# Two instead of three products of the cleared tile at the head of TensorE's program

## What is computed

```python
x = x + _L0_xattn_ref(_layernorm(x), ctx_768, Wq, Wk, Wv, Wo, bo)        # 8 heads of 64
x = x + _L0_ffn_ref(_layernorm(x), ...)                                  # 16 experts, 4 of them chosen in groups, one shared
x = x + _L1_xattn_ref(_layernorm(x), ctx_768, Wq, Wk, Wv, Wo)            # 16 heads of 8
x = x + _L1_ffn_ref(_layernorm(x), ...)                                  # 8 experts, 2 chosen, one shared
```

## Time and profile before

| | |
|---|---|
| median of three runs | 231.79 us |
| the three runs | 231.2, 231.79, 233.03 us |
| the profiled execution, first to last instruction | 230.0 us |
| PE busy | 223.5 us, 97% |
| DVE, ACT, POOL busy | 163.7, 155.3, 126.4 us |

### The profile page before, as it was taken

The page is one execution under the profiler, slowest core; times in us unless marked ns, Lnnn a source line. Parts: engine busy times, 40 slices in busy tenths (PEclk is TensorE's granted clock), DMA queues, the critical chain, the costliest instruction groups (busy, mean ns, idle before and its releaser), DMA issues.

```text
span 230.0 us, 4315 instructions
## 1 busy us (share of the span) xinstructions
PE 223.5 (97%) x1389; PEld 166.7 (72%) x1389; DVE 163.7 (71%) x480; ACT 155.3 (68%) x378; POOL 126.4 (55%) x127
## 2 busy tenths in 40 slices
PE   7999999999999999999999999999999999999994
PEld 3676765965889898889535563588878887888883
DVE  3589984788667863699948983564857775776874
ACT  2579999986679445672689778876365586745561
POOL 2765743899046937767492107209499400996540
PEclk9999999999999999999999999999999999999999
DMA  6890000000029925900600000028000003700002
GB/s 204 211 296 4 1 3 0 0 3 1 3 74 242 362 114 144 221 3 4 217 3 3 3 1 6 0 79 293 0 0 0 3 0 87 284 0 4 0 0 91
DMA packets 10172, 17.04 MB, mean 74 GB/s; under 512 B 3715, under 2 KB 5540, under 8 KB 9766
## 3 DMA queue, kind: packets, MB, share of 16 engines
q1 hardware_dynamic: 9926, 16.45, 23.5%
q10 hardware_dynamic: 224, 0.32, 0.4%
HBM read 16.08 MB, written 0.62 MB: 73 GB/s over the span
## 4 chain that ended last, share of the span: by engine, by line
PE 86%; ACT 6%; DVE 4%; POOL 2%; issue 1%; DVEq 0%; POOLq 0%
PE psum L1175 12%; PE psum L1179 11%; PE psum L1176 11%; PE psum L1348 7%; ACT prob L749 5%; PE psum L1410 5%; PE psum L1356 4%; PE psum L1358 3%; PE psum L1357 3%; PE psum L1466 3%; PE psum L1294 3%; PE psum L1306 3%; PE psum L1431 2%; PE psum L1270 2%; PE psum L1183 2%; PE psum L1454 2%
## 5 line engine op out<-in xcount | busy, mean ns | idle before, releaser
L703 POOL TENSOR_TENSOR act_s<-act_s,spread 128x512 f32<-128x512 f32 x35 | 44.3, 1293 | 20.2 <-DMA spread<-cw 14.5
L1175 PE MATMUL psum<-xT_hi,w_hi 128*128 128x512 f32 x108 | 43.9, 406 | 0.0
L1179 PE MATMUL psum<-xT_lo,w_hi 128*128 128x512 f32 x108 | 42.3, 392 | 0.0
L1176 PE MATMUL psum<-xT_hi,w_lo 128*128 128x512 f32 x108 | 42.2, 391 | 0.0
L798 ACT CAST q<-psum 128x512 fp32r<-128x512 f32 x35 | 20.4, 587 | 20.4 <-PE psum L1358 14.1
L1009 DVE TENSOR_TENSOR q<-psum,q 128x512 fp32r<-128x512 f32 x35 | 23.8, 687 | 13.5 <-ACT q L798 13.2
L788 ACT ACTIVATE act_s<-psum 128x512 f32<-128x512 f32 x39 | 23.0, 597 | 12.3 <-PE psum L1179 7.7
L1146 DVE TENSOR_REDUCE neg_max<-psum 128x2 f32<-128x308 f32 x64 | 26.2, 472 | 4.3 <-PE psum L1410 4.0
L703 POOL TENSOR_TENSOR hid<-hid,spread 128x512 f32<-128x512 f32 x13 | 16.6, 1296 | 18.9 <-DMA spread<-cw 14.6
L652 POOL TENSOR_TENSOR rstd<-vareps,minus_half 128x4 f32<-128x4 f32 x8 | 8.1, 1017 | 34.0 <-DVE vareps L910 34.0
L646 POOL TENSOR_TENSOR w_lo<-w_src,w_hi 128x768 fp32r<-128x768 f32 x12 | 21.7, 1830 | 8.3 <-ACT w_hi L718 8.3
(11 more groups left out here) (171 smaller groups left out, 469.6 us busy)
## 6 DMA issues: line engine op xcount, KB each, us to landing
spread<-cw SPq DMA_DIRECT2D x16, 256.0 KB, 4.9
spread<-cw SPq DMA_DIRECT2D x6, 512.0 KB, 5.7
w_src<-in_w SPq DMA_DIRECT2D x2, 1152.0 KB, 5.1
w_src<-in_w SPq DMA_DIRECT2D x1, 2304.0 KB, 11.6
spread<-cw SPq DMA_DIRECT2D x8, 128.0 KB, 3.0
w<-in_w SPq DMA_DIRECT2D x1, 576.0 KB, 6.6
out<-X SPq DMA_DIRECT2D x4, 128.0 KB, 1.8
wv<-in_wv SPq DMA_DIRECT2D x2, 192.0 KB, 4.7
```

Of the source, the lines that this page charges most:

```text
L703: pool.tensor_tensor(g, g, spread[:, slot, :], ALU.mult).then_inc(weighed, 1)
L1175: pe.matmul(dst, w_hi, xT_hi[:, b, :], start=True, stop=False)
L1176: pe.matmul(dst, w_lo, xT_hi[:, b, :], start=False, stop=False)
L1179: return pe.matmul(dst, w_hi, xT_lo[:, b, :], start=False, stop=True)
```

## The change

The third product of the cleared tile, the one of 256 columns, is left out. The wait for `idle_ready`, the bank and everything behind it stay as they are.

```diff
             pe.wait_ge(idle_ready, 1)
-            for n in (TOK, TOK, TOK // 2):
+            for n in (TOK, TOK):
                 pe.matmul(psum[:, 7, 0:n], act_s[:, 0, 0:P], act_s[:, 0, 0:n], start=True, stop=True)
```

## The result

The changed kernel takes 232.43 us (median of 20 runs), the kernel before 231.56 in as many: ratio 1.004, 95% interval 1.0026 to 1.0054. The forecast was 231.4. The time is inside the stated range (230.7 to 233.3), but the sign is wrong: the change costs 0.9 us where 0.4 was to be won.

The account below looks back on a forecast made before the run. PE, busy 97% of the span, was taken to bound the kernel, its first third at half rate. The lead of 0.41 us less 0.02 at batch 1's transposes gave 0.4: 231.79 to 231.4 us, range 230.7 to 233.3.

Parts of the forecast that it names:

- PE's head is on the path, and the load of wk is late next.: Kernel start: cleared products lie on the chain; without the third, kT waits for wk's load and starts at 5.10 us.
- Nobody reads bank 7 and no semaphore hangs on it, so nothing else goes with it.: Removed product: only 0.85 us of slow PE time goes, with no other effect.
- a lead was there at 15 us and gone at the end: Sign of a wrong prediction: PE's gain, expected to last to the end, seen at 15 us and then lost.
- The rise of the clock at 7.5 us.: During kT: PE goes from 1.2 to 2.4 GHz at a fixed 7.5 us, leaving 0.41 us of the 0.76 us lead.
- The forecast's gain: Whole kernel: 0.4 us faster, 231.4 us; chance 0.5.
- the whole lead remains: Rival at kT: clock rises with the work, PE keeps 0.76 us, gain hardly over 0.5, 231.2 us; chance 0.1.
- the clock rises later: Rival ahead of kT: PE's idle gap delays the clock's rise, 1.1 to 2.1 us slower, 232.9 to 233.9; chance 0.2.
- the lead is eaten: Rival: late wk or vf1 load, or batch 1's tile, leaves 0 to 0.2 us of gain, 231.7 us; chance 0.2.

Follow-up runs that it names:

- e4: Third product left out and the first kT made to wait for the identity's load too, against the kernel before: ratio 1.0077.
- e1: The same change run once more (products of 512, 512 columns), against the kernel before: ratio 1.004.
- f2: Third product left out, four PE instructions given back behind the store by two extra transposes at cwT of batch 1, against the kernel before: ratio 1.0053.
- g1: All three products kept, four PE instructions removed at about 52.5 us (low part of x skipped for two first-gate tiles), against the kernel before: ratio 1.0047.
- g3: Third product left out, two PE instructions given back by doing one transpose of the first xT twice, against the kernel before: ratio 1.0027.
- f1: Third product left out, four PE instructions given back ahead of the store by doubling a small vs product (about 21 us), against the kernel before: ratio 0.9997.
- e2: Third product cut from 256 to 8 columns, as many instructions as before, against the kernel before: ratio 1.0007.
- f4: One product of 512 columns and two of 8, as many instructions as before, against the kernel before: ratio 1.006.

## Why the prediction was wrong, point by point

- *PE's head is on the path, and the load of wk is late next.* Right. The first pass of kT started at 4.81 to 5.07 in the traces with two products that had no added wait, where 5.0 to 5.2 was expected.
- *"Nobody reads bank 7 and no semaphore hangs on it, so nothing else goes with it."* This step failed. Four instructions went with it, and everything behind them moved up in PE's program. The refill that used to run at 60.9 us, ahead of the store of the routing weights, ran at 64.0 to 64.8 (66.1 in e4, whose head is 1.4 us later), on top of it, in every run with two to four instructions less at that point (the change, e1, e4, f2, g1, g3), and the store took 3.16 to 3.59 us there against 1.83 to 1.85 in the six others. f1 and f2 differ in where the four instructions come back (and in what small product brings them), and g1 has the loss without the head. This is shown. Two rows more leave little room for another cause: in all six the first of the five late packets starts within 0.02 us of the refill's end, and the next store of the same size, at 84 to 87 us, takes 1.81 to 1.84 in all twelve traces. In the recorded pair the store lands 1.3 us later, and PE goes from 0.15 us ahead to 0.6 behind: a lead was there at 15 us and gone at the end, one of the signs that the prediction gave for being wrong. That the five packets queued behind the refill on one engine is read from their number, a sixteenth of 80, and from their start at its end; the engine's name isn't in the trace.
- *Why two instructions move the refill by 3.5 us or more*: the cause stays open. It is all or nothing: measured from PE's weight load for the transpose of the routing weights (line 1326, 62.97 in the trace of before), the refill starts 1.8 to 2.2 us ahead in the six runs with the short store and 1.7 to 1.9 us behind in the six with the long one. Two waits of PE's program lie there. One is for the router (the choice of experts), whose last step on DVE (line 1095) ends at 61.02 in the trace of before; the early refills start within 0.3 us of that step's end. The other is for ACT's copy of the transposed weights out of bank 3, which ends at 63.50 in the trace of the change; the late refills start 1.05 to 1.2 us behind that copy. I take it that the place that sets off the refill lay ahead of such a wait and lies behind it now. This is argued from the times, not shown. (The Trainium skill, "Runtime: NRT & Kernel Launch", section "Instruction fetch mechanics", says that a sequencer fetches its program in blocks of 16 KiB, 256 instructions, by a DMA queue of its own, and that crossing a boundary is mostly hidden. The trace agrees with the block's size: 11 packets of queue q8, 0.18 MB together, stand in that of before, for 1389 weight loads and 1389 passes on PE, which is 10.9 such blocks. Hidden it wasn't in the changed kernel, for what it cost was another transfer's time.)
- *The rise of the clock at 7.5 us.* A fixed time was wrong as a rule. With the same two products the last slow weight load was before 4.8 in the trace of the change, and the first fast ones came at 7.02 in f1. With the three products of before, they came at 7.65 in the trace of before and at 4.76 in that of g1. In the trace of the change the lead was 0.15 us, since kT was early and the normalised x was then the last thing waited for. In that of e2 it was 0.4, as forecast, but g1 has the first exponential 0.7 us earlier than the trace of before with the same head, so one trace cannot tell such a lead from the spread of executions. In the medians of e2 and f1, whose intervals reach 0.2 to 0.3% to either side, a lead of 0.4 us (0.17%) can be neither seen nor excluded. The forecast's gain is open in this sense, and with it the rival "the whole lead remains".
- *The rival "the clock rises later"* had the sign, and not for its reason: at two products it isn't visible. With less it is seen, in one trace each: slow weight loads to the end of kT in f4, with a ratio of 1.006, and in e4, where it is a part of the 0.8%.
- *The rival "the lead is eaten"* named the loads of the first 13 us. What ate it lay 50 us later, at a transfer that the prediction didn't look at, since the chain of before held no DMA. A chain tells what ended last, not how near the next thing was: the first `down` had about 0.65 us in hand behind the routing weights (the first `spread` 1.32 us later against the store, PE's wait ahead of `down` 0.66).

No version here is seen to beat the kernel before: e2 and f1, which keep the shorter head and put the refill back, can't be told from it.

## What to carry to other kernels

Before calling an edit free, count the instructions that it takes from or adds to an engine's program, and look in the trace where that engine's instruction packets run and which small transfers with a waiter lie near them. If a ratio can't be explained at the edit, put the instructions back in another place (ahead of the suspected transfer, then behind it): the pair tells place from time in two runs. And a single trace of a start-up phase says little about the clock's rise there: with one and the same head it differed by more than 2 us.

## What was not expected of the hardware

One refill packet, 0.96 to 1.44 us on one of the 16 DMA engines, lengthened a store of 32 KB by 1.3 to 1.75 us (1.84 to 3.16 and 3.59). The column of the granted clock read 1.00 in the stretches where passes ran at half rate. The clock's rise differed by more than 2 us between executions with the same head: with three products, weight loads were fast from 4.76 in the trace of g1 and still slow at 6.93 in that of before.
